# A graph layer's gather ring made two chunks deep, and its edge numbers loaded after transposes instead of sums

## The reference

```
theta = x[dst] - x[src]
w = jax.nn.sigmoid(jax.nn.relu(theta @ W1 + b1) @ W2 + b2)
w_theta = w * theta
agg = jax.ops.segment_sum(w_theta, dst, num_segments=n_nodes)
indeg = jax.ops.segment_sum(jnp.ones((dst.shape[0], 1), x.dtype), dst, num_segments=n_nodes)
return agg + indeg * (x @ W4 + b4)
...
x = _layernorm(x + _L0_gnn_ref(x, src, dst, L0_gnn_W1, ...), axis=-1)
```

## Time and profile before

| what | value |
|---|---|
| median of 3 runs | 5257.63 us (5248.12 to 5259.45) |
| span of the profiled execution | 5257.5 us |
| the run that the span stands nearest to | 5257.63 us |
| TensorE matmuls busy | 4021.0 us (76%) |
| GpSimd busy | 3071.6 us (58%) |
| VectorE busy | 2289.7 us (44%) |
| ScalarE busy | 1222.0 us (23%) |
| mean granted clock of TensorE | 0.842 of full |

### The profile page before, as it was taken

One profiled execution on the slowest core, in us unless ns is written; L12 is line 12 of the kernel. 1 busy time (PEld: TensorE's weight loads), 2 busy tenths in 40 slices (PEclk: granted clock), 3 DMA queues, 4 the chain that ended last, 5 costly groups with the idle time before them and its releaser, 6 DMA issues.

```text
span 5257.5 us, 79790 instructions
## 1 busy us (share of the span) xinstructions
PE 4021.0 (76%) x23554; PEld 2973.8 (57%) x23956; DVE 2289.7 (44%) x9032; ACT 1222.0 (23%) x2536; POOL 3071.6 (58%) x3231
## 2 busy tenths in 40 slices
PE   6777877777778777777777777777777877777776
PEld 4555555555556555555555555555555555555555
DVE  3444444444444444444444444444444444444444
ACT  2222222222222222222222222222222222222222
POOL 5555555556555655655565555655555565655554
PEclk8888888888888888888888887888888888888888
DMA  1111111111111111111111111111111111111111
GB/s 45 44 44 44 45 44 45 44 44 45 43 45 44 45 44 43 45 45 45 43 45 44 43 43 43 45 44 44 44 44 43 44 45 44 45 44 45 45 43 34
DMA packets 187593, 230.45 MB, mean 44 GB/s; under 512 B 105912, under 2 KB 136012, under 8 KB 187572
## 3 DMA queue, kind: packets, MB, share of 16 engines
q0 software_dynamic: 103296, 211.41, 15.5%
q1 hardware_dynamic: 84276, 18.80, 1.7%
HBM read 222.36 MB, written 7.60 MB: 44 GB/s over the span
## 4 chain that ended last, share of the span: by engine, by line
PE 53%; another core or an unknown queue 29%; issue 10%; ACT 6%; DVE 1%; SPq 0%; ACTq 0%; DMA 0%; DVEq 0%
PE ps_hid L399 15%; PE ps_log L407 11%; PE ps_sum L421 10%; PE ps_hid L382 7%; PE ps_srcT L391 5%; ACT hidden L486 3%; PE ps_rel L371 3%; ACT srcT L480 3%; PE ps_win L435 1%; ACT wgt L493 1%; PE ps_sum L415 0%; PE ps_win L429 0%; DVE hot_en L593 0%; ACTq L83 0%
## 5 line engine op out<-in xcount | busy, mean ns | idle before, releaser
L357 POOL DMA_INDIRECT gath<-in_x,src_i x3224 | 3070.9, 953 | 2145.3 <-remote 890.9
L593 DVE SCALAR_TENSOR_TENSOR hot_en<-col_no,rel,wgt 128x128 f32<-128x128 f32 x3224 | 920.2, 347 | 2025.7 <-ACT wgt L493 1498.1
L399 PE MATMUL ps_hid<-srcT,neg_w 128*128 128x512 f32 x1612 | 1081.2, 760 | 663.6 <-ACT srcT L480 421.1
L407 PE MATMUL ps_log<-w,hidden 128*128 128x1 f32 x6448 | 861.0, 255 | 416.2 <-ACT hidden L486 400.9
L407 PEld LDWEIGHTS ps_log<-w,hidden 128*128 128x128 f32 x6448 | 865.4, 209 | 473.8 <-issue 357.2
L421 PE MATMUL ps_sum<-gath,hot_en 128*128 128x129 f32 x6448 | 1015.8, 307 | 0.0
L584 DVE TENSOR_SCALAR_CACHE_REDUCE hot_ne<-ps_rel,row_no 128x512 bf16<-128x512 f32 x806 | 604.4, 750 | 781.7 <-remote 402.3
L486 ACT ACTIVATE hidden<-ps_hid,b_col 128x512 f32<-128x512 f32 x806 | 553.8, 687 | 1564.7 <-PE ps_hid L399 1028.9
L421 PEld LDWEIGHTS ps_sum<-gath,hot_en 128*128 128x128 f32 x6448 | 897.9, 215 | 0.0
L480 ACT COPY srcT<-ps_srcT 128x512 f32<-128x512 f32 x806 | 471.0, 584 | 1568.1 <-remote 1051.8
L399 PEld LDWEIGHTS ps_hid<-srcT,neg_w 128*128 128x128 f32 x1612 | 303.4, 235 | 704.3 <-ACT srcT L480 442.2
(11 more groups left out here) (67 smaller groups left out, 1015.7 us busy)
## 6 DMA issues: line engine op xcount, KB each, us to landing
gath<-in_x,src_i POOLq DMA_INDIRECT x3224
window<-in_x SPq DMA_DIRECT2D x116, 64.0 KB
out<-yout SPq DMA_DIRECT2D x116, 64.0 KB
first_i<-in_dst SPq DMA_DIRECT2D x116, 0.5 KB
src_i<-in_src SPq DMA_DIRECT2D x115, 14.0 KB
dst_i<-in_dst SPq DMA_DIRECT2D x115, 14.0 KB
w<-in_L_gnn_W SPq DMA_DIRECT2D x2, 64.0 KB
b_rows<-in_L_gnn_b SPq DMA_DIRECT2D x1, 64.0 KB
```

What stands on the lines that cost most here:

```text
L357: nc.gpsimd.indirect_dma_start(gath[0:parts, t, 0:F], None, x, bass.IndirectOffsetOnAxis(ap=src_i[0:parts, k.parity, t:t + 1], axis=0))\
L399: nc.tensor.matmul(ps_hid[b][:, :], neg_w1[:, :], srcT[:, b, :], start=False, stop=True)\
L407: last = nc.tensor.matmul(ps_log[:, t:t + 1], hidden[:, b, t * P:(t + 1) * P], w2[:, :], start=True, stop=True)
L593: last = nc.vector.scalar_tensor_tensor(hot_en[:, b, t, :], col_no[:, :], rel[:, k.parity, e:e + 1], wgt[:, b, t:t + 1].to_broadcast([P, P ...
```

## The change

`gath` gets a second chunk's room, by the chunk's parity, and the semaphores `gathered` are doubled with it. TensorE adds `NB` to `summed` once at its start, and the two waits on VectorE are raised by `NB` to match. GpSimd's wait keeps its number, so that it now asks for batch j of the chunk two before. SyncE's wait ahead of `load_chunk(nxt(k))` is for `srcT_ready` at `k.c * NB` in the place of `summed` at `k.c * NB`: all of chunk k-1 transposed, where it was all of chunk k-1 summed.

```diff
-        gath = sb("gath", [P, K, GW])
+        gath = sb("gath", [P, 2, K, GW])
...
-        gathered = [sem(f"gathered{n}") for n in range(NB)]
+        gathered = [[sem(f"gathered{q}_{n}") for n in range(NB)] for q in range(2)]
...
                 if not is_last(k):
-                    wait(sp, summed, k.c * NB)
+                    wait(sp, srcT_ready, k.c * NB)
                     load_chunk(sp, nxt(k))
...
                 for j in range(batches):
                     if not is_first(k):
-                        pool.wait_ge(summed, (k.c - 1) * NB + j + 1)
+                        wait(pool, summed, (k.c - 1) * NB + j + 1)
                         pool.sem_inc(pool_gate, 1)
                     for t in range(j * B, (j + 1) * B):
                         nc.gpsimd.indirect_dma_start(
-                            gath[0:parts, t, 0:F], None, x,
+                            gath[0:parts, k.parity, t, 0:F], None, x,
                             bass.IndirectOffsetOnAxis(ap=src_i[0:parts, k.parity, t:t + 1], axis=0))\
-                            .then_inc(gathered[j], 16)
+                            .then_inc(gathered[k.parity][j], 16)
...
-                wait(pe, gathered[j], 16 * B * (k.c + 1))
+                wait(pe, gathered[k.parity][j], 16 * B * k.nth)
...
+            pe.sem_inc(summed, NB)
             transpose_window(Chunk(0, 0, 1))
...
-                wait(dve, summed, k.c * NB + j - 1)
+                wait(dve, summed, (k.c + 1) * NB + j - 1)
...
-                wait(dve, summed, k.c * NB + batches)
+                wait(dve, summed, (k.c + 1) * NB + batches)
...
-            v.memset(gath[:, :, F:F + 1], 1.0)
+            v.memset(gath[:, :, :, F:F + 1], 1.0)
```

More of the change, by code:

```diff
@@ L388, in transpose_src @@
                 wait(pe, srcT_copied, k.c * NB + j - 1)
-                wait(pe, gathered[j], 16 * B * (k.c + 1))
+                wait(pe, gathered[k.parity][j], 16 * B * k.nth)
                 for t in range(B):
-                    last = nc.tensor.transpose(ps_srcT[b][:, t * P:(t + 1) * P], gath[:, j * B + t, 0:F],
+                    last = nc.tensor.transpose(ps_srcT[b][:, t * P:(t + 1) * P], gath[:, k.parity, j * B + t, 0:F],
                                                ident[:, :])
@@ L421, in add_up @@
                     last = nc.tensor.matmul(ps_sum[:, 0:F + 1], hot_en[:, b, t, :],
-                                            gath[:, j * B + t, 0:F + 1],
+                                            gath[:, k.parity, j * B + t, 0:F + 1],
                                             start=False, stop=(stop and t == B - 1))
```

## The result

The changed kernel takes 6721.06 us (median of four runs, 6717.48 to 6725.44) against 5254.94 us for the kernel before, measured beside it (four runs, 5248.12 to 5259.45). The ratio is 1.2787, 95% interval 1.2769 to 1.2805. The change costs 1466 us, over a quarter.

The account below looks back on a forecast made before the run. Unbroken runs of gathers were taken to hold back reports of TensorE's finished work. Terms sum to 57.0 us a chunk, 11.3 more than now, 113 times, plus 35 at the start: 5257.5 + 1277 + 35 = 6570 us, range 5500 to 7300.

Parts of the forecast that it names:

- step 2: TensorE's work on a batch, seven a chunk: its transposes were to come 2.2 us after the released sum.
- step 1: TensorE step done during the 24-gather run; its sum, which batch 6's gathers need, was to be held until the run's end.
- until the reports come: From the end of the 24-gather run to the release of TensorE's held semaphores: 1.6 us.
- step 2 to step 6's transposes: TensorE after the release: four more steps at the free pace of 3.96 us, 15.8 us.
- window, carry: The window product and carry, once in each chunk's cycle: 1.4 us.
- half clock: TensorE's clock at half of full after the hold, slowing one step: 2.6 us.
- last four gathers: The chunk's second run, four gathers after the run of 24, slowing a TensorE step by 0 to 3.0 us, taken as 1.5.
- the load: SyncE's load of source numbers, the only gate ahead of a chunk's gathers: between 0 and 3.8 us, taken as 2.2.
- Rival 1: Faster: GpSimd's waits, not gathers, hold TensorE back; GpSimd's issue bounds at 35.0 us a chunk, 4080 us, up to 4700; chance 0.13.
- Rival 2: No change: each gather costs the same hold, 0.6 us, wherever it stands; 5260 us; chance 0.03.
- rival 3: Mildly slower: reports seep through, two more steps done in the 24-gather run; 49.1 us a cycle, 5680 us; chance 0.12.
- Rival 4: Slower than forecast: step 1 not done either, clock at half for two more steps; 66.2 us, 7600 us; chance 0.04.

Follow-up runs that it names:

- run 1: Changed kernel with the source-number load back behind the same sums as in the kernel before, so only the two-chunk ring: 7101.4 us, ratio 1.3701 to the kernel before.
- run 3: Changed kernel, with GpSimd waiting before each batch of four gathers for the landing of the batch before: 5793.01 us, ratio 1.1179 to the kernel before.
- run 4: Changed kernel, with GpSimd pausing for landed rows only every eight gathers: 5288.04 us, ratio 1.0203 to the kernel before.
- run 8: Kernel before, with GpSimd waiting only before every second batch, for both sums, so runs are eight long: 5644.92 us, ratio 1.0900.
- run 5: Changed kernel with each gather fetching 16 in place of 128 floats per row, an eighth of the bytes: 6729.48 us, ratio 1.3019 to the kernel before.
- run 6: Changed kernel with each indirect gather replaced by GpSimd's plain transfer of 128 fixed rows: 3313.48 us, ratio 0.6410 to the kernel before.
- run 7: Changed kernel with plain transfers of fixed rows issued by SyncE and none by GpSimd: 3311.71 us, ratio 0.6407 to the kernel before.
- run 11: Changed kernel with each gather fetching 32 rows in place of 128: 6698.87 us, ratio 1.2968 to the kernel before.
- run 10: Changed kernel with every second gather replaced by GpSimd's plain transfer of the same size: 3314.5 us, ratio 0.6417 to the kernel before.
- the last comparison: Changed kernel plus one plain GpSimd transfer behind every four gathers: 4569.65 us; the kernel before, timed beside it, 4099.95 us; ratio 1.1146.
- run 2: Kernel before with only the earlier load of the source numbers: 5154.45 us, ratio 0.9947.
- run 9: Changed kernel with a one-column memset by GpSimd after every gather, each waiting for the one before: 6682.12 us, ratio 1.2932 to the kernel before.

## Why the prediction was right

The forecast was 6570 us, and 6721.06 was measured, 2.3% above it and inside the range of 5500 to 7300.

**The bound and its mechanism.** Right: runs of gathers hold back TensorE's reports. Runs 1, 3, 4 and 8 move the time by where GpSimd stops, with each engine's work left as it is. Runs 5, 6, 7 and 11 show that it is the indirect instruction, not bytes, rows or queue. One point was put too strongly, that almost nothing is reported until the run ends: in the cycle shown four waits of ScalarE and VectorE were released during the run, and they carried TensorE as far as step 2's transposes, at 2621.05. The next logits had to wait for the end of the run. By what means it holds the reports is not shown.

**The cut of the runs.** Right: 24 and 4, since the sum of step 1 is held until the run ends. "How the run is cut hardly matters" was too strong: unbroken runs of 28 (run 1) took 7101 us, though that kernel also starts each run later, a whole chunk's sums being done first. Its cycle is 28 x 1.25 + 26.8 less the gap of 0.3 = 61.5 us.

**The terms of the cycle**, forecast 57.0 us, measured 58.07 us in the cycle shown:

| term | forecast | measured |
|---|---|---|
| 24 gathers | 29.7 | 29.66 (2603.93 to 2633.59) |
| until the reports come | 1.6 | 4.47 (to 2638.06) |
| step 2 to step 6's transposes, with window, carry, half clock, last four gathers | 23.5 | 21.05 (to 2659.11) |
| the load | 2.2 | 2.89 (to 2662.00) |

The mis-sized term is the second. I took it from a run of eight and passed over the first chunk's 2.6 us; after 24 or 28 gathers it is 4.5 to 4.8 us (the cycle above and run 1). The third was 2.4 us too high, so the errors partly cancel. It holds 2.2 us from the released sum to step 2's transposes, and these were made at 2621.05, long before the release; without the 2.2 it is 21.3, near the 21.05 measured. At the start the first run has 56 gathers, as reckoned, though TensorE made some headway in it (the copy at 44.20). 113 cycles of 58.07 in the place of 45.7 and these 35 us make 5257.5 + 1398 + 35 = 6690 us; the 30 us to the span measured are 0.3 us a cycle, from one cycle taken as the mean.

**What the profile was to show.** Shown: gathers 1.25 us apart in runs of 24, gaps behind them, TensorE at 61%, a clock of 0.73. The gap of about 20 us ends with the load, after 18.46 us. Not shown: one wait of ScalarE's copy of 15 to 25 us that ends 1.6 to 2.6 us after the run. The copy waited 9.8 us in the mean (898.6 / 92), in the cycle shown it was let go in mid-run, and the long waits were spread over sigmoid, relu and logits, to 4.47 us after the run.

**The rivals.** Rival 1 (the waits hold TensorE back) is refuted by run 3, where more waits made the kernel faster, and by run 1. Its price of 4080 us, though, is near what the kernel before took in the last comparison. What the change costs without the hold wasn't measured. There, by this reckoning, the gathers would be the bound with or without a second chunk of room, and I would expect no loss, but no run here shows it. Rival 2 is refuted by run 10. In rival 3's favour reports did seep through, at 2616.84 and 2630.96 among them, but they brought no further step to its end before the run was over. Rival 4 didn't come: step 1's sum was begun at 2611.52, early in the run, and the cycle is 58.07 us, not 66.2. The rule of the Trainium skill (SBUF — State Buffer, "SBUF: two separate sides"), that TensorE and ScalarE never wait on anyone at their ports, isn't contradicted by these runs: what came late was a report of finished work, and nothing shows a port as its cause. It just doesn't bound what gathers can cost TensorE, which stood for 16.78 us in one run of them.

**What stays open:** which resource holds the reports; why the hold was absent in the last comparison; and whether the slower pace or the plain transfer between removes it in run 10. Since the hold can be absent without any edit, runs 6, 7 and 10 prove something only because others beside them were held: the kernel before, at 5155 to 5190 us in all its runs of the one comparison and 5149 to 5178 in the other, and runs 5, 9 and 11. Of the versions that compute the reference, only the early load alone (run 2) beat the kernel before that was timed beside it, by 0.5%.

## What to carry to other kernels

More buffers can cost time. Before you relax a wait, look at what else happens while it lasts: here GpSimd's waits cut its runs of indirect gathers, and in those pauses the other engines got the reports that they were waiting for. When idle time is put down to an unseen release, line up the ends of these waits with the ends of other engines' runs. And compare versions only with a base that was timed beside them.

## What the runs showed of the hardware

- An indirect gather occupies GpSimd for 0.95 us, and the next starts 0.30 us later, whether it fetches 128 rows of 512 bytes or of 64 (951 ns); with 32 rows it is 872 ns. A plain transfer of the same 128 rows takes 0.54 us.
- An unbroken run of such gathers holds back reports from TensorE. During it they come singly, up to 14 us apart in the cycle shown, and the rest together behind its end: 1.6 us after eight gathers, 2.6 to 4.8 us after 24 to 28, and 5.9 us after a run of gathers of 32 rows. TensorE's own instructions go on until one needs an answer (to the transposes at 2621.05, with the report of logits begun at 2610.63 still out).
- In turns with plain transfers, 14 indirect gathers in 25 us held back nothing, at 1.87 us from one indirect gather to the next.
- The same kernel on the same chip took 5167.61 us in one comparison and 4099.95 in the next, with granted clocks of 0.84 to 0.85 and of 0.985. Within each comparison its runs agree to about 1%.
